# A bias that moves from its own product into a spare row of the aggregate's operands, and a last product cut in even halves

## Time and profile before

| | us |
|---|---|
| runs before (3) | 245.59, 245.69, 247.01 |
| the profiled execution, its own time | 243.86 |
| its span, first to last instruction | 242.1 |
| around the span (the difference) | 1.76 |
| TensorE busy | 232.5 |
| VectorE busy | 181.2 |
| ScalarE busy | 65.6 |

### The profile page before, as it was taken

How to read it: one execution, slowest core, us unless ns; L and a number is a source line. 1 busy time by engine, 2 the same in 40 slices (tenths; PEclk the granted TensorE clock), 3 DMA queues, 4 the chain that set the end, 5 groups by cost and what they waited for, 6 DMA issues and landing times.

```text
span 242.1 us, 4104 instructions
## 1 busy us (share of the span) xinstructions
PE 232.5 (96%) x1695; PEld 193.2 (80%) x1695; DVE 181.2 (75%) x338; ACT 65.6 (27%) x86; POOL 16.6 (7%) x36
## 2 busy tenths in 40 slices
PE   7699999999999999999999999999999999999990
PEld 7588778777787778887887878788899999887890
DVE  3769859799996877796799698739529789655564
ACT  3742425245153043102102202313315533100000
POOL 8020000000000000000020020002000000011111
PEclk9999999999999999999999999999999999999998
DMA  6888620305004200000000000003700870002111
GB/s 184 231 211 140 210 83 3 89 12 169 0 2 176 91 0 3 0 8 1 3 5 3 0 8 0 3 5 106 240 4 0 230 202 0 1 20 67 43 42 42
DMA packets 10376, 15.95 MB, mean 66 GB/s; under 512 B 2930, under 2 KB 3680, under 8 KB 10354
## 3 DMA queue, kind: packets, MB, share of 16 engines
q1 hardware_dynamic: 10172, 15.49, 22.7%
q10 hardware_dynamic: 182, 0.16, 0.2%
HBM read 14.22 MB, written 1.28 MB: 64 GB/s over the span
## 4 chain that ended last, share of the span: by engine, by line
PE 91%; issue 3%; DMA 3%; DVE 1%; SPq 1%; ACT 0%; POOL 0%; POOLq 0%; DVEq 0%
PE ps L1007 89%; DMA stage<-in_L_gnn_W_self 3%; PE ps L1095 1%; PE ps L1014 1%; SPq L354 1%; ACT wring L488 0%; POOL small L471 0%; DVE small L991 0%; DVE t2buf L990 0%; POOLq L177 0%; DVE ybuf L983 0%; DVEq L177 0%; DVE small L972 0%; DVE small L974 0%
## 5 line engine op out<-in xcount | busy, mean ns | idle before, releaser
L1007 PE MATMUL ps<-wring,hT 128*125 128x512 f32 x300 | 72.8, 398 | 1.6 <-ACT wring L488 1.5
L1007 PEld LDWEIGHTS ps<-wring,hT 128*125 128x125 f32 x300 | 54.6, 185 | 14.7 <-ACT wring L488 1.7
L1007 PE MATMUL ps<-T_hi,AT_hi 125*125 125x512 f32 x100 | 40.3, 403 | 0.0
L1007 PE MATMUL ps<-T_lo,AT_hi 125*125 125x512 f32 x100 | 39.4, 394 | 0.0
L706 DVE TENSOR_TENSOR eqp<-iota_p,pairs 128x1638 f16<-128x1638 f16 x25 | 25.1, 1005 | 2.6 <-issue 1.3
L1007 PE MATMUL ps<-T_hi,AT_lo 125*125 125x512 f32 x100 | 26.0, 403 | 0.0
L516 ACT CAST AT_hi<-ps 128x1500 fp32r<-128x1500 f32 (+1 forms) x10 | 12.3, 1234 | 48.7 <-PE ps L1007 48.6
L1007 PEld LDWEIGHTS ps<-kw,eqp 128*128 128x128 f16 x650 | 19.4, 97 | 6.5 <-issue 6.3
L1007 PE MATMUL ps<-kw,eqp 128*128 128x40 f16 (+1 forms) x650 | 21.8, 190 | 0.3 <-issue 0.2
L1007 PEld LDWEIGHTS ps<-T_lo,AT_hi 125*125 125x125 f32 x100 | 18.6, 186 | 4.2
L1007 PEld LDWEIGHTS ps<-T_hi,AT_hi 125*125 125x125 f32 x100 | 18.5, 185 | 4.2
(11 more groups left out here) (125 smaller groups left out, 278.5 us busy)
## 6 DMA issues: line engine op xcount, KB each, us to landing
stage<-in_L_gnn_W_rel SPq DMA_DIRECT2D x8, 512.0 KB, 3.7
stage<-in_L_gnn_W_ffn SPq DMA_DIRECT2D x8, 512.0 KB, 4.3
x<-in_x SPq DMA_DIRECT2D x5, 224.0 KB
x_again<-in_x SPq DMA_DIRECT2D x5, 224.0 KB
stage<-in_L_gnn_W_self SPq DMA_DIRECT2D x2, 512.0 KB, 7.1
out<-ybuf SPq DMA_DIRECT2D x4, 224.0 KB
g_bc<-in_L_gnn_ln_g SPq DMA_DIRECT2D x2, 256.0 KB, 6.5
b_bc<-in_L_gnn_ln_b SPq DMA_DIRECT2D x2, 256.0 KB, 7.2
```

The lines of the kernel that those rows point to most:

```text
L1007: return nc.tensor.matmul(o, l, r, start=start, stop=stop, skip_group_check=True)
```

## The change

- The bias is made part of T. Row 126 (SUMS) of T_hi[r, s] is the high part of b_rel[r], row 126 of T_lo the low part, and row 125 is zero in both. `brel` now has 40 rows, 20 with the bias and 20 with zeros, and `brel_low` beside it. Four DMAs (SyncE, L401 of the changed kernel) copy them from SBUF into T, each 20 rows of 512 into one partition. They are issued behind the load of unit 7 and a wait for `brel_lo`.
- The aggregate's matmuls read 127 rows (KT) where they read 125, and the first waits for `T_bias`.
- `biases(c)` becomes `degrees(c)`: the 512-column matmul goes, the 2-column one stays, and `sums` has two groups of rows (52 partitions), so 10 DMAs where there were 15.
- b_rel is loaded once: 4 DMAs where there were 12.
- HALVES are 256 and 256 columns where they were 384 and 128.

```
-    SUM_ROWS = [0, 32, 64]
+    KT = SUMS + 1
+    SUM_ROWS = [0, 32]
...
-    brel = sb("brel", [P, D], F32R, 200)
+    brel = sb("brel", [2 * TR, D], F32R, 200)
+    brel_low = sb("brel_low", [2 * TR, D], F32R, 191.5)
...
-        HALVES = [(0, 3 * D // 4), (3 * D // 4, D)]
+        HALVES = [(0, D // 2), (D // 2, D)]
...
-                for row, half in zip(SUM_ROWS, (0, 1, 0)):
+                for row, half in zip(SUM_ROWS, (0, 1)):
...
-            for row in SUM_ROWS:
-                for r in range(R):
-                    sp.dma_start(brel_raw[row + r * NT:row + (r + 1) * NT, :],
-                                 b_rel[r:r + 1, :].broadcast_to([NT, D])).then_inc(brel_in, 16)
+            for r in range(R):
+                sp.dma_start(brel_raw[r * NT:(r + 1) * NT, :], b_rel[r:r + 1, :].broadcast_to([NT, D])).then_inc(brel_in, 16)
             for u in range(STAGES, U_REL):
                 load(u)
+                if u == 2 * STAGES + 1:
+                    sp.wait_ge(brel_lo, 1)
+                    for T, b in ((T_hi, brel), (T_lo, brel_low)):
+                        for row, q in ((SUMS, 0), (SUMS - 1, TR)):
+                            sp.dma_start(f32(T[row:row + 1, :, :, :].rearrange("p r s d -> p (r s) d")),
+                                         f32(b[q:q + TR, :])).then_inc(T_bias, 16)
...
-            a.copy(brel[0:BK, :], brel_raw[0:BK, :]).then_inc(brel_hi, 1)
+            a.copy(brel[:, :], brel_raw[:, :]).then_inc(brel_hi, 1)
...
-            v.tensor_tensor(brel[SUM_ROWS[2]:BK, :], brel_raw[SUM_ROWS[2]:BK, :], f32(brel[SUM_ROWS[2]:BK, :]),
-                            ALU.subtract).then_inc(brel_lo, 1)
+            v.tensor_tensor(brel_low[:, :], brel_raw[:, :], f32(brel[:, :]), ALU.subtract).then_inc(brel_lo, 1)
...
+                    if q == 0 and c == 0:
+                        pe.wait_ge(T_bias, 16 * 4)
...
-                    w = AT[c % 2][0][0:TN, q, :]
-                    mm(o, w, T_hi[0:TN, r, s, :], q == 0)
-                    mm(o, w, T_lo[0:TN, r, s, :], False)
+                    w = AT[c % 2][0][0:KT, q, :]
+                    mm(o, w, T_hi[0:KT, r, s, :], q == 0)
+                    mm(o, w, T_lo[0:KT, r, s, :], False)
...
-            def biases(c):
-                if c == 0:
-                    pe.wait_ge(brel_lo, 1)
-                pe.wait_ge(sums_in[c % 2], 48 * (c // 2 + 1))
+            def degrees(c):
+                pe.wait_ge(sums_in[c % 2], 32 * (c // 2 + 1))
                 if c >= 1:
                     pe.wait_ge(deg_ev, c)
-                w = sums[0:BK, c % 2, :]
-                mm(agg_bank(c)[0:TN], w, brel[0:BK, :], False)
-                mm(DEG[0:TN, 0:2], w, sum_ones[0:BK, :], True, True).then_inc(deg_ps, 1)
+                mm(DEG[0:TN, 0:2], sums[0:BK, c % 2, :], sum_ones[0:BK, :], True, True).then_inc(deg_ps, 1)
```

More of the change, by code:

```diff
@@ L128, in gnn_layer @@
     order = sb("order", [P, EC], F32, 57.25)
-    brel_raw = sb("brel_raw", [P, D], F32, 58)
+    brel_raw = sb("brel_raw", [2 * TR, D], F32, 58)
     x1T_hi = sb("x1T_hi", [P, KD, NT, TP], F32R, 80)
@@ L227, in gnn_layer @@
         brel_lo = sem("brel_lo")
+        T_bias = sem("T_bias")
         xpad = sem("xpad")
@@ L513, in A_high @@
                     act.wait_ge(agg_ps, n - 1)
-                    act.wait_ge(sums_in[n % 2], 48 * (n // 2))
+                    act.wait_ge(sums_in[n % 2], 32 * (n // 2))
                 i0, nb = GROUPS[g][0], len(GROUPS[g])
@@ L544, in _ @@
             high_part(3)
-            act.wait_ge(brel_in, 16 * len(SUM_ROWS) * R)
-            a.copy(brel[0:BK, :], brel_raw[0:BK, :]).then_inc(brel_hi, 1)
+            act.wait_ge(brel_in, 16 * R)
+            a.copy(brel[:, :], brel_raw[:, :]).then_inc(brel_hi, 1)
             high_part(4)
@@ L628, in _ @@
             link(v.memset(small[:, 0:45], 0.0))
-            v.memset(f32(sum_ones[0:SUM_ROWS[2], :]), 1.0)
-            v.memset(f32(sum_ones[SUM_ROWS[2]:P, :]), 0.0)
+            v.memset(f32(sum_ones[:, :]), 1.0)
             row_mean(0)
@@ L1119, in aggregate_lo @@
                         pe.wait_ge(A_b, group_of(c, NG - 1))
-                    i = mm(o, AT[c % 2][1][0:TN, q, :], T_hi[0:TN, r, s, :], False, q == TR - 1)
+                    i = mm(o, AT[c % 2][1][0:KT, q, :], T_hi[0:KT, r, s, :], False, q == TR - 1)
                 return i
-            def biases(c):
-                if c == 0:
-                    pe.wait_ge(brel_lo, 1)
-                pe.wait_ge(sums_in[c % 2], 48 * (c // 2 + 1))
+            def degrees(c):
+                pe.wait_ge(sums_in[c % 2], 32 * (c // 2 + 1))
                 if c >= 1:
                     pe.wait_ge(deg_ev, c)
-                w = sums[0:BK, c % 2, :]
-                mm(agg_bank(c)[0:TN], w, brel[0:BK, :], False)
-                mm(DEG[0:TN, 0:2], w, sum_ones[0:BK, :], True, True).then_inc(deg_ps, 1)
+                mm(DEG[0:TN, 0:2], sums[0:BK, c % 2, :], sum_ones[0:BK, :], True, True).then_inc(deg_ps, 1)
             def cols_of(t, k, c0, n):
@@ L1236, in stages @@
                     aggregate_hi(c, range(14, TR))
-                    biases(c)
+                    degrees(c)
                     if n + 1 < NT:
```

## The result

The changed kernel took 249.06 us, the median of 22 runs (246.21 to 252.6), beside 245.63 us for the kernel before (22 runs, 243.53 to 247.43). The ratio is 1.0127, 95% interval [1.0099, 1.0155]: slower by 1.3%. Forecast was 244.1 us, 0.6% less.

What follows compares the result with a forecast made beforehand. TensorE, 91% of the chain, was taken as the bound, except two places in the aggregate where VectorE is. Savings of 0.69 + 0.86 = 1.55 us from 245.69 gave 244.1 us, range 243.1 to 245.3.

Steps and rivals of the forecast that it cites:

- The wait for `T_bias` and the four copies: SyncE's copies of the bias into T: issued from 42.8, hidden by units 6 to 9, cost 0.
- The rival for slower: Slow copies into one partition hold up unit 8's load on the same queue: 262 us at the long end, chance 0.03.
- The point from which it decides: Copies taking 20 us (63 - 43) would begin delaying unit 8's load, each us beyond costing one on TensorE.
- 3 × 0.23 = 0.69: Aggregate: removed bias products save 0.23 us each in tiles 0, 3 and 4, nothing in 1 and 2.
- stays where it was: Aggregate: the 2-column product with its two waits remains in place, with no added cost counted.
- 0.86: Last row tile: 256 and 256 columns save 0.76 us to the moments' end plus 0.10 at the second store.
- The rival by which columns alone count: Last row tile: columns alone set matmul time down to 128, halves gain nothing on TensorE; 0.52 in all, 245.2 us, chance 0.02.
- Fewer DMAs: Start: four b_rel loads instead of twelve send unit 3's load out 4.0 us earlier, worth 0; the rest 0 to 0.1.
- Predicted -1.55: Whole kernel: 0.69 for the bias products plus 0.86 for the last row tile, giving 244.1 us; chance 0.64.

Runs made afterwards that it cites:

- copies_late: The changed kernel with the four copies into T issued behind the load of unit 8 instead of unit 7: 243.91 us, ratio 0.9956 to the kernel before.
- late_deg84: The changed kernel with the four copies behind the load of unit 8 and 84 rows instead of 52 in the degree's matmul: 244.06 us, ratio 0.9950.
- bias_late_deg84: The changed kernel with copies behind unit 8's load, the old 384 and 128 column halves, and 84 rows in the degree's matmul: 245.37 us, ratio 1.0000.
- halves_alone: The kernel before with only the last row tile cut into 256 and 256 columns: 245.14 us, ratio 0.9976.

## Why the prediction was wrong

**The step that failed: "The wait for `T_bias` and the four copies", put at "cost 0, hidden by units 6 to 9".** The rival for slower had the right culprit and the wrong victim. I asked who stands behind the copies on SyncE's queue (the load of unit 8) and who needs their data (the first aggregate), found 20 and 50 us of room, and these two were indeed not late. The victim stands on no queue of the program and in no row of its order: VectorE at its jump, and by my reading of q14 its code, which is itself a DMA and shares the 16 engines. The kernel of before showed it, as 1.27 us of idle time by "issue" ahead of `eqp` at 47.49 and as an instruction packet of q14 just ahead of it, in us 45 to 46; I did not read either. The point from which it decides was not 20 us of copies: it was enough that they were issued from 45.31, 3.3 us ahead of the moment at which VectorE falls idle (45.21 + 3.38 = 48.59), and still ran then. Their size was not the error. I took some 2.4 us each, 9.6 in all, and from the first issue to the last increment of `T_bias` it was 8.7 us (45.31 to 53.97), and 9.5 in copies_late (55.05 to 64.50).

The Trainium skill has the rule, in "Runtime: NRT & Kernel Launch", section "Instruction fetch mechanics": a taken branch with a target outside the two pages held forces a DMA fetch of the target page before execution goes on. The trace agrees in that VectorE stands idle at the jump, 1.27 us even when nothing else moves, with a packet of instructions just ahead. The page gives no price, and none for busy DMA engines; here that was 4.88.

**"3 × 0.23 = 0.69" for the bias products: -0.08 instead.** The mechanism was right to the row: late_deg84 shows the seven matmuls and the step behind them in tile 1 taking 123.76 - 121.73 = 2.03 us, where the prediction said 2.0 for 1.79, with the wait for `kw` now named in the row, and bias_late_deg84 gains 0.68 in all. What failed is the sentence on the 2-column product that "stays where it was": its cost was put at nothing more. It stayed, but fell from 84 rows to 52, and so under 65. I had weighed 127 rows against 125, and not this one. Each of the five then costs some 0.26 us more (0.32 + 0.20 less 0.23 + 0.03), which takes back the 0.23.

The Trainium skill's "TensorEngine Tiling (Array Packing)" states in "Key Properties" that a change of tiling mode drains TensorE, and in "When to Use Tiling" that row tiling goes with 64 rows or fewer. The traces have their border between 64 and 65 too. The page does not say that a matmul of 64 rows or fewer is such a change of mode; that is my inference, and what the runs show is the border and the two gaps.

**"0.86" for the last row tile: right, 0.9.** 0.118 us for a matmul of 256 columns (predicted 0.120), VectorE's add 0.42 (0.424), moments 0.43. The rival by which columns alone count, 0.52 in all, fell: halves_alone shows 0.9. The prediction set a rule of the Trainium skill against this part, and used it wrongly: in "TensorE: Matmul & The Clock Gate", section "Back-to-back issue gap", that formula is for an isolated matmul, and the same section says that it is too low at few columns, with some 81 ns for 128 columns in a stream. The trace agrees that 128 columns cost more than by the formula, and has 107 ns.

**Fewer DMAs: 0 where it can be read.** ScalarE waited for loads of `stage` twice in this stretch before, 2.9 us in all, and not once after, but TensorE does not run earlier for it: from its 24 matmuls at 15.63 to the block at 42.72 it takes 27.09 us before, and 27.08 after (18.24 to 45.32). The 0.24 us just behind that block may belong here; no run tells. The start differs between executions by more than this part could be worth.

**The sum.** Predicted -1.55. By the traces: -0.9 for the halves, +0.08 for the bias, +3.62 for the jump, +1.37 for the clock that fell behind it. That is +4.2 in the profiled execution; the medians differ by 3.43 and the ratio gives 1.3%, 3.1 us. It may be that not every execution pays all of it: over the 22, the mean granted clock lies between 0.969 and 0.992, with 0.981 in the profiled one. One trace does not show how they divide.

**What stays open.** The code packet explains 1.9 of the 3.6 us at the jump (2.35 less 0.48). Most of the rest lies behind its end (2.85 us to `eqp` where it was 1.41), and also vanishes with the copies moved or spread. That `T_bias` gets its increments up to 2.4 us behind the copies' last packet fits a word of landing that is held up too, for the code as for the copies. It was not tried apart, and nor was the other candidate at this place: ahead of the jump VectorE reads `flag` from SBUF (`value_load`), and no run has that read without the jump. That the copies into one partition cause the idle time is shown; by which of these ways all of it comes is not.

## What to carry to other kernels

Where an engine's program jumps, look for its idle time by "issue" and the instruction packets beside it, and keep copies of many pieces into one partition away from it; such a copy that has 20 us of room should not be issued 3 us ahead of a jump. When a matmul's operand shrinks, look at what stands next to it: here a 2-column matmul of 65 or 84 rows beside others of 84 to 128 cost nothing, and one of 64 or 52 as much as a whole product of 512 columns. With both mended, late_deg84, the change is worth having: 0.5% faster than before.

## What had not been expected of the hardware

- Copies from 20 partitions into one partition keep the DMA engines busy at a poor rate at their end (share 0.46 at 33 GB/s), and their last word of landing comes 2.2 to 2.6 us behind their last packet. The same bytes into 20 partitions were still moving at the jump too (0.51 and 0.21 in us 46 to 48), and did not hold it up.
- One 8 KB packet of code (as I read q14) took 0.48 us on idle DMA engines and 2.35 us beside such copies, and VectorE stood still for 4.88 us.
- Waits of 2.37 and 1.19 us on TensorE were followed by a granted clock of 0.50 to 0.66 over four us, dearer by 1.37 us; waits of 0.35 and 0.74 were not.
- A 2-column matmul with 64 rows between matmuls of 127 and 128 rows costs 0.26 us more than one with 65 rows.
